# A recommender's gated experts on one core: no second layer in fp32, x rounds and second layers in one unrolled order

## The chip, the core and the metric

The kernel runs on one core of a Trainium2 chip. TensorE (PE in the profile) multiplies matrices into PSUM; VectorE (DVE), ScalarE (ACT) and GpSimd (POOL) work on tiles in SBUF and PSUM; SyncE (SP) issues transfers. Each engine runs its own instructions in order and waits for others by semaphores. The metric is the time of one execution on the device in microseconds (us).

## The reference

```
mask = x.sum(-1) != 0                                   # x: 512 x 64 x 768, fp32
p = softmax(where(mask, einsum('bld,d->bl', x, aw), -inf))
feature = einsum('bl,bld->bd', p, x)                    # 512 x 768
g_h = relu(einsum('bd,hdk->bhk', feature, gW1) + gb1)   # 4 heads, 384 wide
gate = softmax(einsum('bhk,hke->bhe', g_h, gW2) + gb2)[b, D]     # 8 experts
h1 = relu((einsum('bd,edk->ebk', feature, eW1) + eb1) * inv1 + bn1_b)   # 8 x 768 x 768
h2 = relu((einsum('ebk,eko->ebo', h1, eW2) + eb2) * inv2 + bn2_b)       # 8 x 768 x 384
rep = einsum('be,ebo->bo', gate, h2)
out = softmax((einsum('bo,hoc->bhc', rep, hW) + hb)[b, D])
```

## The kernel before

**The x rounds.** x is read once, 100 MB, in 32 rounds of 16 batch rows (four chunks of 768 KB). Eight rounds make a block of 128 batch rows, two blocks a chunk of 256. SyncE loads a round into one of four ring places when the round that held it is done (`feat_added`). In a round VectorE computes eight score tiles (`score_tile`, L637, 128x768 each) and ScalarE eight row sums for the mask (`sum_rows`, L439). Then, one round later, the softmax of the round follows: VectorE masks the scores (L645, L649), PE transposes them (`turn_scores`, L950), VectorE takes the negative maximum (L656), ScalarE the exponential (L446), VectorE normalises (L663, L665), PE transposes back (`turn_probs`, L955), VectorE places the probabilities as columns of `pwin` (`place_probs`, L678), and PE multiplies them with x (`add_features`, L972, sixteen fp32 matmuls, which the trace shows as 32 records). After eight rounds the sums are copied (`copy_rows`), transposed (`turn_features`) and split into a high and a low part in fp32r.

**The weights.** A panel is 384 columns of one weight matrix, a unit half of its rows (576 KB). GpSimd loads units. A split unit is cut by ScalarE into a high part in fp32r (`split_hi`, L423) and by VectorE into a low part (`split_lo`, L625), and PE takes three fp32r products for each tile (L908 to L910), 27 matmuls of 256 columns for a unit. ScalarE then reads the result through a relu. For a second layer h1 is also split, by VectorE (`split_h1`, L699, L701). The second layers of experts 0 to 5 of chunk 0 are the exception: their twelve units are not split, and PE multiplies raw h1 with raw weights in fp32 (`w2raw`, L940), nine matmuls for a unit, which the trace shows as 18 records.

**The order.** Three rounds' thirds and the splits of units 0 and 1 stand at the front. A loop over two blocks follows on every engine (`x_round`), with PE's `turn_scores` of the next round between the two halves of `add_features`. Then 64 slots are written out, one unit each: eight gate units of chunk 0, the experts 0 to 7 of chunk 0 with six units each (first layer in four, second in two), with the gate units of chunk 1 inside the last expert. Slots 0 to 44 each carry a third of one of the remaining x rounds (`x_third`). VectorE and ScalarE split unit s + 2 in slot s. `head_logits(0)` stands after the last slot. A second loop does chunk 1, four experts to an iteration, in the order of its layers. The vectors of parameters are transposed in slot 0 (`turn_params`, `set_params`).

Of the kernel before, what the change touches and what calls it, by code (L numbers as in the profile page):

```python
# [17 lines left out]

# [14 lines left out]
BODY = 4  # L33
EU = 6


def rec_kernel(nc, x, D, aw, gW1, gb1, gW2, gb2, eW1, eb1, bn1_g, bn1_b, eW2, eb2, bn2_g, bn2_b, hW, hb, out):
# [8 lines left out]
    GU = 2 * H  # L46
    BU = BODY * EU
    ITERS = E // BODY
    assert 2 * L == P and KT == 2 * KU and HD == UNIT_COLS and ITERS == CB
    assert MT * (NCH * GU + EU * E) // 2 % ZB == 0 and MT * (BU // 2) % ZB == 0  # L50
    assert GU % RAW == 0 and BU % RAW == 0 and BU % SPLIT == 0

# [6 lines left out]
    with ExitStack() as ctx:  # L59
# [8 lines left out]


# [60 lines left out]

        prm = rows[:, 0:2 * P].rearrange("p (a n) -> p a n", a=2)
# [7 lines left out]
        exps = soft_ps[0:ROUND_TILES, 2 * P:3 * P].rearrange("t (h l) -> t h l", h=2)  # L139

# [3 lines left out]

# [10 lines left out]
        zeroed = sem("zeroed")  # L155
        link_dve = sem("link_dve")
        params_ready = sem("params_ready")
# [16 lines left out]

        turned = sem("turned")
        turned_hi = sem("turned_hi")
        turned_read = sem("turned_read")
# [10 lines left out]
        gl_ready = sem("gl_ready")  # L188
        gmax_ready = sem("gmax_ready")
        gexp_ready = sem("gexp_ready")  # L190
        gate_ready = sem("gate_ready")
        gateT_ready = sem("gateT_ready")
# [11 lines left out]

        def tiles(it, panel, m):

            return it * (MT * BU // 2) + (MT * panel + m + 1)

        def wait_unit_used(eng, it, u0):

            if u0 % 2 == 0:
                eng.wait_ge(half_used, it * (BU // 2) + (u0 // 2 + 1))
            else:
                eng.wait_ge(z_ready, tiles(it, u0 // 2, MT - 1))


        GATES = [[(c, n, None, None) for n in range(GU)] for c in range(NCH)]
        EXPERTS = [[(0, None, q, k) for k in range(EU)] for q in range(E)]

        ORDER = (GATES[0] + [u for expert in EXPERTS[:-1] for u in expert] + EXPERTS[-1][:2] + GATES[1]
                 + EXPERTS[-1][2:])
        SLOTS = len(ORDER)

        def gate_at(c):

            return ORDER.index((c, 0, None, None))  # L230

        def expert_at(c, q, k):

            return SLOTS + EU * q + k if c else ORDER.index((0, None, q, k))

        SPLIT_FROM = 6

        def is_split(u0):  # L240
            if u0 >= SLOTS:
                return True
            _, n, q, k = ORDER[u0]
            return n is not None or k < EU - 2 or q >= SPLIT_FROM

        def splits(it, u0):

            return it * BU + sum(is_split(v) for v in range(u0 + 1))

        def h1_splits(it, c, q, t):  # L250

            return it * (KT * BODY) + (KT * (q + (E if c else 0) - SPLIT_FROM) + t + 1)

        def raw_slot(u0):

            return (splits(0, u0) - 1) % RAW

        def turned_gate(c):

            return (soft_ps if c else turn_ps)[0:E, 0:CHUNK]  # L260

        def wait_loaded(eng, it, u0):

            if is_split(u0):
                eng.wait_ge(w_loaded[raw_slot(u0)],
                            it * (16 * BU // RAW) + 16 * ((splits(0, u0) - 1) // RAW + 1))
            else:
                eng.wait_ge(w2_loaded[u0 % 2], 16 * (ORDER[u0][2] + 1))

        N1, N2 = E * KT, E * HT  # L270


        FEAT_TURN = [(2 * CB + 2) * c + (c > 0) for c in range(NCH)]
        PRM_TURN = 2 * CB

# [3 lines left out]
        GATE_TURN = [FEAT_TURN[c] + 2 * CB + (c == 0) for c in range(NCH)]  # L279

        def turned_feat(c, j, g):

            if c == 0:
                return z_ps[:, g, 0:KU * P]
            return (soft_ps if (j, g) == (CB - 1, 1) else turn_ps)[:, 0:KU * P]

        FEAT_READ = [2 * CB * c + (c > 0) for c in range(NCH)]

        SCORES, BLOCK_THIRDS = 3, 3 * BLOCK_ROUNDS

        def to_score(third):
            return range(SCORES * third, min(SCORES * third + SCORES, ROUND_TILES))


        MASK_AT, MAX_AT, NORM_AT, PLACE_AT, EXP_AT = 0, 1, 3, 4, 3

        LEAD = 3
        SLOT_THIRD = LEAD + BLOCK_THIRDS
        FIRST_SPREAD = BLOCK_ROUNDS
        ROUNDS = (1 + CB) * BLOCK_ROUNDS

        BLOCK_END = {3 * (BLOCK_ROUNDS * (j + 2) + 1) + 2 - SLOT_THIRD: j for j in range(CB)}

        BLOCK_GATED = [(t - GU) // EU for t in sorted(BLOCK_END)]

        TURN_SLOT = {(j, g): t + (g if j == 0 else 0) for t, j in BLOCK_END.items() for g in range(2)}

        GATE_COPY, GATE_PICK, GATE_NORM, GATE_SET = ([gate_at(c) + GU + n for c in range(NCH)] for n in (1, 2, 3, 4))

        block = ctx.enter_context(nc.Block())


        @block.sync  # L320
        def _(sp):
            def load_round(b, r, wait):

                if wait:
                    sp.wait_ge(feat_added, b * BLOCK_ROUNDS + (r + 1 - RING_ROUNDS))
                for j in range(CG):

                    rr, jj = divmod(r * CG + j - IN_FLIGHT, CG)
                    if (wait and j) or (rr >= 0 and not wait):
                        sp.wait_ge(x_loaded[rr % RING_ROUNDS][jj], b * 32 + 16 * (rr // RING_ROUNDS + 1))  # L330
                    sp.dma_start(xring[:, r % RING_ROUNDS, j, :, :],
                                 x_v[b, r, :, j, :, :]).then_inc(x_loaded[r % RING_ROUNDS][j], 16)

            for r in range(RING_ROUNDS):
                load_round(0, r, False)
# [12 lines left out]
            for r in range(RING_ROUNDS, BLOCK_ROUNDS):  # L348
                load_round(0, r, True)
            with sp.Fori(1, NBLK) as b:  # L350
                for r in range(BLOCK_ROUNDS):
                    load_round(b, r, True)
# [4 lines left out]


        @block.gpsimd
        def _(pool):  # L360
            nc.gpsimd.memset(ident[:, :], 0.0).then_inc(ident_zero, 1)
            pool.wait_ge(ident_zero, 1)
            nc.gpsimd.affine_select(out=ident[:, :], in_=ident[:, :], compare_op=ALU.not_equal, fill=1.0,
                                    base=0, pattern=[[-1, P]], channel_multiplier=1).then_inc(ident_ready, 1)

            def load_unit(it, u0, src):
                if is_split(u0):
                    if u0 >= RAW:

                        pool.wait_ge(lo_ready, splits(it, u0) - RAW)  # L370
                    pool.dma_start(wraw[:, raw_slot(u0), :, :], src).then_inc(w_loaded[raw_slot(u0)], 16)  # L371
                else:


                    wait_unit_used(pool, it, u0 - EU)
                    pool.dma_start(w2raw[:, u0 % 2, :, :], src).then_inc(w2_loaded[u0 % 2], 16)

            def gate_unit(u0, n):
                head, half = divmod(n, 2)
                load_unit(0, u0, gW1_v[head, :, KU * half:KU * half + KU, :])  # L380

            def expert_unit(it, u0, expert, k):
                panel, half = divmod(k, 2)
                ks = slice(KU * half, KU * half + KU)
                if panel < 2:
                    src = eW1_v[expert, :, ks, UNIT_COLS * panel:UNIT_COLS * (panel + 1)]
                else:
                    src = eW2_v[expert, :, ks, :]
                load_unit(it, u0, src)


            for r, units in ((0, range(AHEAD)), (CB * BLOCK_ROUNDS, range(AHEAD, RAW))):
                pool.wait_ge(x_loaded[r % RING_ROUNDS][CG - 1], 16 * (r // RING_ROUNDS + 1))
                for n in units:
                    gate_unit(n, n)
            for s in range(RAW, SLOTS):
                _, n, q, k = ORDER[s]
                if n is not None:
                    gate_unit(s, n)
                else:  # L400
                    expert_unit(0, s, q, k)
            with pool.Fori(0, ITERS) as it:
                for n in range(BU):
                    expert_unit(it, SLOTS + n, it * BODY + n // EU, n % EU)

            for n in range(AHEAD):
                expert_unit(0, SLOTS + BU * ITERS + n, 0, n)
            for n in range(AHEAD):
                wait_loaded(pool, 0, SLOTS + BU * ITERS + n)


        @block.scalar
        def _(act):
            act.dma_start(aw_bc[:, :], aw.partition_broadcast(P)).then_inc(aw_loaded, 16)

            def split_hi(it, u0):
                if not is_split(u0):
                    return

                wait_loaded(act, it, u0)  # L420
                if u0 >= SPLIT:
                    wait_unit_used(act, it, u0 - SPLIT)
# [725 lines left out]
```

## Time and profile before

| what | value |
|---|---|
| median of three runs | 636.95 us (636.2 to 636.99) |
| span of the profiled execution | 636.0 us |
| PE busy | 532.7 us, 84% |
| VectorE busy | 495.2 us, 78% |
| ScalarE busy | 441.0 us, 69% |
| HBM read | 168.5 MB, 265 GB/s over the span |

The span runs from the first to the last instruction of the profiled execution; the time of that execution alone was not kept, and the median of the runs is 0.95 us longer than the span. Busy shares are averages over stages with different limits, so they have to be read by stage. PEclk is the clock that TensorE was granted, 1.00 for 2.4 GHz and 0.50 for 1.2 GHz.

### The profile page before, as it was taken

Reading aid. Unit: us, or ns where it says so; the run is one execution under the profiler, and the core shown is the slowest. Engines: PE = TensorE matmul, PEld = TensorE weight load, DVE = VectorE, ACT = ScalarE, POOL = GpSimd, SP = SyncE. Lnnn points to the kernel's source line nnn. Section 1 sums busy time; section 2 is a strip of 40 time slices with the busy share of each in tenths; the row PEclk is TensorE's granted clock in tenths of the full one; section 3 lists DMA queues with packets and bytes.
Section 4 is the critical chain, followed back from the end, with each engine's and each line's share of the span. In section 5 each row is a group of like instructions: output and inputs, shape, how many; then the busy total and the mean of one; then the engine's idle time right before and its main releaser. Section 6 shows DMA issues by size and latency. Waiting matters only on the chain.

```text
span 636.0 us, 12288 instructions
## 1 busy us (share of the span) xinstructions
PE 532.7 (84%) x4153; PEld 422.3 (66%) x4153; DVE 495.2 (78%) x1085; ACT 441.0 (69%) x939; POOL 82.6 (13%) x120
## 2 busy tenths in 40 slices
PE   0075564444799999999999999999999999999994
PEld 0011111111498778787787778898899999999994
DVE  5599988999799799879798977534767677676774
ACT  5588878889698787888788885454445565555652
POOL 1000000001011210202020111111112212222210
PEclk9998885889799999999999999999989999999998
DMA  8999997999998989899989935354446655565540
GB/s 311 405 363 377 364 374 296 341 357 377 409 365 300 365 304 381 334 392 330 349 314 377 350 112 150 112 176 134 142 113 184 185 162 176 184 185 167 168 148 1
DMA packets 52618, 169.10 MB, mean 266 GB/s; under 512 B 4829, under 2 KB 5073, under 8 KB 52573
## 3 DMA queue, kind: packets, MB, share of 16 engines
q1 hardware_dynamic: 36012, 100.88, 41.7%
q0 software_dynamic: 16416, 67.25, 32.9%
q10 hardware_dynamic: 144, 0.39, 0.3%
q8 instruction: 26, 0.43, 0.3%
q14 instruction: 20, 0.16, 0.1%
HBM read 168.50 MB, written 0.00 MB: 265 GB/s over the span
## 4 chain that ended last, share of the span: by engine, by line
PE 69%; DVE 16%; issue 10%; DMA 3%; ACT 1%; DVEq 0%; SPq 0%; POOL 0%; ACTq 0%
PE z_ps L908 17%; PE z_ps L909 16%; PE z_ps L910 16%; DVE prod_out L637 10%; PE feat_ps L972 7%; PE z_ps L940 7%; DMA xring<-in_r_x_dram 2%; PE turn_ps L1039 2%; DMA wraw<-in_L_rec_gW_dram 1%; PE turn_ps L1008 1%; DVE score L637 1%; DVE neg_max L656 1%; DVE wlo L625 1%; DVE pwin L678 0%; PE turn_ps L1050 0%
## 5 line engine op out<-in xcount | busy, mean ns | idle before, releaser
L637 DVE CUSTOM_DVE_ANT_0 prod_out<-xring,aw_bc 128x768 bf16<-128x768 f32 x256 | 234.1, 948 | 5.4 <-DMA xring<-in_r_x_dram 4.7
L439 ACT ACTIVATE copy_out<-xring 128x768 bf16<-128x768 f32 x256 | 211.7, 828 | 5.8 <-DMA xring<-in_r_x_dram 5.8
L908 PE MATMUL z_ps<-feat_hi,whi 128*128 128x256 f32 x720 | 209.0, 290 | 1.5 <-DVE feat_lo L689 1.5
L909 PE MATMUL z_ps<-feat_lo,whi 128*128 128x256 f32 x720 | 204.2, 284 | 0.0
L910 PE MATMUL z_ps<-feat_hi,wlo 128*128 128x256 f32 x720 | 204.2, 284 | 0.0
L625 DVE TENSOR_TENSOR wlo<-wraw,whi 128x1152 fp32r<-128x1152 f32 x102 | 138.2, 1355 | 83.4 <-ACT whi L423 82.4
L423 ACT ACTIVATE whi<-wraw 128x1152 fp32r<-128x1152 f32 x102 | 118.3, 1160 | 86.5 <-PE z_ps L910 79.2
L908 PEld LDWEIGHTS z_ps<-feat_hi,whi 128*128 128x128 f32 x720 | 138.6, 193 | 15.8 <-issue 12.8
L909 PEld LDWEIGHTS z_ps<-feat_lo,whi 128*128 128x128 f32 x720 | 138.7, 193 | 0.0
L910 PEld LDWEIGHTS z_ps<-feat_hi,wlo 128*128 128x128 f32 x720 | 138.6, 192 | 0.0
L972 PE MATMUL feat_ps<-xring,pwin 128*32 128x384 f32 x1024 | 112.1, 573 | 12.1 <-DVE pwin L678 12.1
L371 POOL DMA_DIRECT2D wraw<-in_L_rec_eW_dram x86 | 64.3, 748 | 232.9 <-DVE wlo L625 226.3
L470 ACT ACTIVATE h<-z_ps,bias,scale 128x256 f32<-128x256 f32 x96 | 52.6, 561 | 33.7 <-PE z_ps L910 33.1
L972 PEld LDWEIGHTS feat_ps<-xring,pwin 128*32 128x32 f32 x1024 | 32.3, 120 | 60.3 <-issue 42.0
L950 PE MATMUL soft_ps<-ident,masked 128*8 128x128 f32 x32 | 9.6, 301 | 57.8 <-DVE masked L649 57.8
L908 PE MATMUL z_ps<-h_hi,whi 128*128 128x256 f32 x180 | 51.1, 284 | 0.0
L909 PE MATMUL z_ps<-h_lo,whi 128*128 128x256 f32 x180 | 50.9, 283 | 0.0
L910 PE MATMUL z_ps<-h_hi,wlo 128*128 128x256 f32 x180 | 50.9, 283 | 0.0
L950 PEld LDWEIGHTS soft_ps<-ident,masked 128*8 128x8 f32 x32 | 2.7, 84 | 72.1 <-DVE masked L649 71.3
L940 PE MATMUL z_ps<-h,w2raw 128*128 128x256 f32 x216 | 48.3, 379 | 0.0
L439 ACT ACTIVATION_READ_ACCUMULATOR copy_out<-xring 128x1 f32 x256 | 47.8, 187 | 0.0
L940 PEld LDWEIGHTS z_ps<-h,w2raw 128*128 128x128 f32 x216 | 40.1, 190 | 5.7
(99 smaller groups left out, 427.8 us busy)
## 6 DMA issues: line engine op xcount, KB each, us to landing
xring<-in_r_x_dram SPq DMA_DIRECT2D x128, 768.0 KB, 8.2
wraw<-in_L_rec_eW_dram POOLq DMA_DIRECT2D x86, 576.0 KB, 4.4
wraw<-in_L_rec_gW_dram POOLq DMA_DIRECT2D x16, 576.0 KB, 6.1
w2raw<-in_L_rec_eW_dram POOLq DMA_DIRECT2D x12, 576.0 KB, 4.6
aw_bc<-in_L_rec_aw_dram ACTq DMA_DIRECT2D x1, 384.0 KB, 5.5
w2raw<-in_L_rec_gW_dram SPq DMA_DIRECT2D x1, 48.0 KB
h<-in_L_rec_eb_dram SPq DMA_DIRECT2D x1, 24.0 KB
h<-in_L_rec_bn_g_dram SPq DMA_DIRECT2D x1, 24.0 KB
```

What stands on the lines that cost most here:

```text
L371: pool.dma_start(wraw[:, raw_slot(u0), :, :], src).then_inc(w_loaded[raw_slot(u0)], 16)
L423: nc.scalar.activation(whi[:, u0 % SPLIT, :, :], wraw[:, raw_slot(u0), :, :], ACT.Copy).then_inc(hi_ready, 1)
L439: nc.scalar.activation(copy_out[:, t % 2, :], xring[:, r % RING_ROUNDS, j, i, :], ACT.Copy, accum_out=rowsum[:, r % 2, t:t + 1]).then_inc( ...
L470: nc.scalar.activation(h1[:, t, :], z_ps[:, (MT * panel + m) % ZB, 0:CHUNK], ACT.Relu, bias=bias[:, col], scale=scale[:, col]).then_inc(z_ ...
L625: nc.vector.tensor_tensor(wlo[:, u0 % SPLIT, :, :], wraw[:, raw_slot(u0), :, :], whi[:, u0 % SPLIT, :, :].bitcast(F32), ALU.subtract).then ...
L637: nc.vector.tensor_tensor_reduce(out=prod_out[:, t % 2, :], in0=xring[:, r % RING_ROUNDS, j, i, :], in1=aw_bc[:, :], scale=1.0, scalar=0.0 ...
L908: nc.tensor.matmul(psum_tile, w_hi, a_hi, start=first, stop=False)
L909: nc.tensor.matmul(psum_tile, w_hi, a_lo, start=False, stop=False)
L910: return nc.tensor.matmul(psum_tile, w_lo, a_hi, start=False, stop=last)
L940: last = nc.tensor.matmul(z, w2raw[:, half, k, cols], h1[:, kk, :], start=(kk == 0), stop=(kk == KT - 1))
L972: last = nc.tensor.matmul(feat_ps[32 * j:32 * j + 32, half, 0:DM // 2], pwin[:, 2 * j + i, at:at + 32], xring[:, r % RING_ROUNDS, j, i, DM ...
L1039: last = nc.tensor.matmul(logit_ps[32 * head:32 * head + E, :], gW2_sb[:, HT * head + m, :], h2[:, m, :], start=(m == 0), stop=(m == HT - ...
```

## The change

- The whole program is unrolled; the two loops are gone.
- No unit is multiplied in fp32 (`NATIVE = 0`): all second layers are split and take three fp32r products, those of experts 0 to 5 of chunk 0 too, with `split_h1`, which now works on three tiles (128x768) at a time.
- The panels of an expert come in another order: the second layer of expert q - 1 (kind "c") stands between the two first-layer panels ("a", "b") of expert q, in both chunks. The gate panels of chunk 1 stand after the last expert of chunk 0.
- The weights of units 0 to 3 are loaded when round 15 of x is there, and units 0 and 1 are split at the end of round 16, no longer ahead of the rounds.
- In an x round `place_probs` moves from VectorE to ScalarE, the exponential writes `prob` in SBUF and no longer PSUM, and `turn_scores`, `turn_probs` and `add_features` of a round stand one after the other on PE. `add_features` moves from the second third of a round to the first, and the feature transposes use `feat_ps`.
- The parameters are transposed in round 10 and set before slot 0. `head_logits(0)` moves to twelve slots after the first gate unit of chunk 1.

```diff
-BODY = 4
-EU = 6
+NATIVE = 0
+THIRDS = 3
...
+        for c in range(NCH):
+            PANELS += [(c, "g", h) for h in range(H)]
+            native = NATIVE if c == 0 else 0
+            for q in range(native):
+                PANELS += [(c, "a", q), (c, "b", q), (c, "c", q)]
+            for q in range(native, E):
+                PANELS += [(c, "a", q)] + ([(c, "c", q - 1)] if q > native else []) + [(c, "b", q)]
+            PANELS += [(c, "c", E - 1)]
...
+            for r in range(FIRST_ROUNDS + 1):
+                sum_rows(r, range(0, 4))
+                if r:
+                    softmax_exp(r - 1)
+                sum_rows(r, range(4, 7))
+                if r:
+                    place_probs(r - 1)
+                sum_rows(r, range(7, ROUND_TILES))
+                if r == FIRST_ROUNDS:
+                    split_hi(0)
+                if r and r % BLOCK_ROUNDS == 0:
+                    copy_rows(r // BLOCK_ROUNDS - 1)
+                if r == FIRST_ROUNDS:
+                    split_hi(1)
...
+                nc.vector.tensor_copy(h1_hi[:, ks, :], h1[:, ks, :]).then_inc(h1_hi_ready, 1)
+                dve.wait_ge(h1_hi_ready, h1_count(c, q, half))
+                nc.vector.tensor_tensor(h1_lo[:, ks, :], h1[:, ks, :], h1_hi[:, ks, :].bitcast(F32),
+                                        ALU.subtract).then_inc(h1_ready, 1)
...
-            with pe.Fori(0, CB) as it:
-                turn_scores(it, 0)
-                for r in range(BLOCK_ROUNDS):
-                    turn_probs(it, r)
-
-                    add_features(it, r, r + 1 if r < BLOCK_ROUNDS - 1 else None)
-                for g in range(2):
-                    turn_features(it, it, 0, 0, g)
+            for r in range(FIRST_ROUNDS):
+                turn_scores(r)
+                turn_probs(r)
+                add_features(r)
+                if r % BLOCK_ROUNDS == BLOCK_ROUNDS - 1:
+                    turn_features(r // BLOCK_ROUNDS)
```

On PE at the end of the first block, before (`masked` are the scores, `prob` the probabilities, `feat_ps` the sums of a block; x8 is half of a round's products):

```order
L950 MATMUL soft_ps<-ident,masked 8x128
L972 MATMUL feat_ps<-xring,pwin 32x384 x8
L955 MATMUL soft_ps<-ident,prob 128x128
L972 MATMUL feat_ps<-xring,pwin 32x384 x16
L984 REGISTER_ALU
L993 MATMUL z_ps<-ident,rows 128x128 x6
```

The same place on PE now:

```order
L859 MATMUL soft_ps<-ident,masked 8x128
L863 MATMUL soft_ps<-ident,prob 128x128
L876 MATMUL feat_ps<-xring,pwin 32x384 x16
L889 MATMUL feat_ps<-ident,rows 128x128 x6
L859 MATMUL soft_ps<-ident,masked 8x128
```

The score transpose of a round stood between the halves of the round before and now stands behind the whole of it.

On ScalarE in a round of the first stage, now (`copy_out` and `rowsum` are the row sums; before, no row of `pwin` stands on this engine):

```order
L412 ACTIVATE copy_out,rowsum<-xring 128x768 x5
L419 ACTIVATE prob,expsum<-soft_ps,neg_max 8x64 x2
L412 ACTIVATE copy_out,rowsum<-xring 128x768 x3
L430 ACTIVATE pwin<-soft_ps 64x8 x2
L412 ACTIVATE copy_out,rowsum<-xring 128x768 x5
```

The placement stands behind the seventh sum of the next round (the last of five belongs to the round before).

On VectorE in the slots of the experts that carry x rounds, before, in two slots of expert 0 whose units ahead are not split (`prod_out` is a score tile):

```order
L656 TENSOR_REDUCE neg_max<-soft_ps 8x2
L637 ISA prod_out,score<-xring,aw_bc 128x768
L637 ISA score 128x1
L637 ISA prod_out,score<-xring,aw_bc 128x768
L637 ISA score 128x1
L637 ISA prod_out,score<-xring,aw_bc 128x768
L637 ISA score 128x1
L663 RECIPROCAL recip<-expsum 8x2
L665 TENSOR_TENSOR prob<-soft_ps,recip 8x128
L637 ISA prod_out,score<-xring,aw_bc 128x768
```

VectorE in two such slots now:

```order
L608 TENSOR_REDUCE neg_max<-soft_ps 8x2
L581 TENSOR_TENSOR wlo<-wraw,whi 128x1152
L646 CAST h1_hi<-h1 128x768
L648 TENSOR_TENSOR h1_lo<-h1,h1_hi 128x768
L593 ISA prod_out,score<-xring,aw_bc 128x768
L593 ISA score 128x1
L593 ISA prod_out,score<-xring,aw_bc 128x768
L593 ISA score 128x1
L593 ISA prod_out,score<-xring,aw_bc 128x768
L593 ISA score 128x1
L614 RECIPROCAL recip<-expsum 8x2
L616 TENSOR_TENSOR prob<-prob,recip 8x128
```

Every slot now has a low part of a weight unit, and two of every six slots the split of one half of h1.

## Rows read from the trace of the kernel before

**Rows 1.** The page, part 4: the chain that ended last, by engine.
```profile
PE 69%; DVE 16%; issue 10%; DMA 3%; ACT 1%; DVEq 0%; SPq 0%; POOL 0%; ACTq 0%
```

**Rows 2.** Windows by stage: length, busy us of each engine, PEclk, DMA share, GB/s.
```profile
25.96:157.79 131.83, 71.08 (x500) 19.08 (x500) 126.26 (x348) 110.67 (x304) 0.65 (x2) 0.83 0.95 359
157.79:171.21 13.42, 8.27 (x56) 2.88 (x56) 10.03 (x30) 8.39 (x22) 1.45 (x3) 0.75 1.02 405
171.21:220.80 49.59, 49.59 (x404) 42.22 (x405) 44.30 (x108) 42.65 (x97) 8.56 (x12) 1.00 0.94 346
220.80:383.03 162.23, 160.62 (x1241) 128.01 (x1241) 141.71 (x320) 133.03 (x309) 24.60 (x33) 1.00 0.88 323
383.03:463.06 80.03, 78.23 (x633) 69.03 (x632) 44.30 (x75) 38.98 (x60) 12.53 (x19) 1.00 0.48 147
463.06:628.59 165.53, 163.40 (x1313) 159.61 (x1312) 115.14 (x179) 94.63 (x124) 32.88 (x44) 0.99 0.53 158
```

**Rows 3.** Timeline of VectorE in one round: start, us, engine, line, operation, tiles.
```profile
57.06 0.96 DVE L637 CUSTOM_DVE_ANT_0 prod_out<-xring,aw_bc 128x768 bf16<-128x768 f32 x1
...
61.92 0.28 DVE L656 TENSOR_REDUCE neg_max<-soft_ps 8x2 f32<-8x128 f32 x1
...
64.07 0.28 DVE L665 TENSOR_TENSOR prob<-soft_ps,recip 8x128 f32<-8x128 f32 x1
...
65.15 0.34 DVE L678 COPY pwin<-soft_ps 64x8 f32<-64x8 f32 x2
...
65.52 0.96 DVE L637 CUSTOM_DVE_ANT_0 prod_out<-xring,aw_bc 128x768 bf16<-128x768 f32 x1
```

**Rows 4.** Timeline of VectorE at the start: chunks 0 and 3, first split, round 1.
```profile
7.93 0.96 DVE L637 CUSTOM_DVE_ANT_0 prod_out<-xring,aw_bc 128x768 bf16<-128x768 f32 x1 [4.66 <-DMA xring<-in_r_x_dram]
...
13.69 0.96 DVE L637 CUSTOM_DVE_ANT_0 prod_out<-xring,aw_bc 128x768 bf16<-128x768 f32 x1
...
22.19 1.36 DVE L625 TENSOR_TENSOR wlo<-wraw,whi 128x1152 fp32r<-128x1152 f32 x1 [6.65 <-ACT whi L423]
...
25.96 0.95 DVE L637 CUSTOM_DVE_ANT_0 prod_out<-xring,aw_bc 128x768 bf16<-128x768 f32 x1
```

**Rows 5.** Timeline of ScalarE in the same round: exponential, next two sums.
```profile
62.24 0.27 ACT L446 ACTIVATE soft_ps<-soft_ps,neg_max 8x64 f32<-8x64 f32 x1 [1.17 <-DVE neg_max L656]
...
62.83 0.83 ACT L439 ACTIVATE copy_out<-xring 128x768 bf16<-128x768 f32 x1
...
63.66 0.83 ACT L439 ACTIVATE copy_out<-xring 128x768 bf16<-128x768 f32 x1
```

**Rows 6.** Timeline of PE: two half bursts and the two whole bursts.
```profile
61.32 2.79 PE L972 MATMUL feat_ps<-xring,pwin 128*32 128x384 f32 x16
...
69.67 1.50 PE L972 MATMUL feat_ps<-xring,pwin 128*32 128x384 f32 x16
...
90.93 4.48 PE L972 MATMUL feat_ps<-xring,pwin 128*32 128x384 f32 x32 [0.82 <-DVE pwin L678]
...
163.63 4.29 PE L972 MATMUL feat_ps<-xring,pwin 128*32 128x384 f32 x32 [0.67 <-DVE pwin L678]
```

**Rows 7.** Timeline of PE: starts of two split units, then of two fp32 units.
```profile
242.66 0.36 PE L908 MATMUL z_ps<-feat_hi,whi 128*128 128x256 f32 x1
...
246.00 0.36 PE L908 MATMUL z_ps<-feat_hi,whi 128*128 128x256 f32 x1
...
255.55 4.05 PE L940 MATMUL z_ps<-h,w2raw 128*128 128x256 f32 x18
...
259.54 4.05 PE L940 MATMUL z_ps<-h,w2raw 128*128 128x256 f32 x18
```

**Rows 8.** Groups by form: count, busy us, mean ns, idle before and releaser.
```profile
L625 DVE TENSOR_TENSOR wlo<-wraw,whi 128x1152 fp32r<-128x1152 f32 x102 | 138.2, 1355 | 83.4 <-ACT whi L423 82.4 <-DVE gateT L812 0.2
L423 ACT ACTIVATE whi<-wraw 128x1152 fp32r<-128x1152 f32 x102 | 118.3, 1160 | 86.5 <-PE z_ps L910 79.2 <-DMA wraw<-in_L_rec_gW_dram 6.9 <-PE z_ps L940 0.4
...
L699 DVE CAST h_hi<-h 128x256 fp32r<-128x256 f32 x60 | 17.9, 298 | 3.6 <-ACT h L470 2.6
...
L725 DVE TENSOR_TENSOR rep<-rep,h 128x768 f32<-128x768 f32 x16 | 15.3, 958 | 0.5
```

More of the change, by code:

```diff
@@ L67, in sem @@
             return ctx.enter_context(nc.semaphore(name))
+        PANELS = []
+        for c in range(NCH):
[6 more added lines that the diff above has]
+            PANELS += [(c, "c", E - 1)]
+        UNITS = [(c, kind, q, half) for c, kind, q in PANELS for half in range(2)]
@@ new lines, in rec_kernel, with is_native, panel_of, unit_of @@
+        SLOTS = len(UNITS)
+        PANEL_AT = {p: n for n, p in enumerate(PANELS)}
+        def is_native(c, q):
+            return c == 0 and q < NATIVE
+        def panel_of(c, kind, q):
+            return PANEL_AT[(c, kind, q)]
+        def unit_of(c, kind, q, half):
+            return 2 * PANEL_AT[(c, kind, q)] + half
+        def is_split(u):
+            c, kind, q, _ = UNITS[u]
+            return kind != "c" or not is_native(c, q)
+        SPLITS = []
+        for u in range(SLOTS):
+            SPLITS.append((SPLITS[-1] if SPLITS else 0) + is_split(u))
@@ new lines, in rec_kernel, with raw_slot, split_slot, tiles @@
+        SPLIT_UNITS = [u for u in range(SLOTS) if is_split(u)]
+        def raw_slot(u):
+            return (SPLITS[u] - 1) % RAW
+        def split_slot(u):
+            return (SPLITS[u] - 1) % SPLIT
+        def tiles(panel, m):
+            return MT * panel + m + 1
+        SPLIT_EXPERTS = [(c, q) for c in range(NCH) for q in range(E) if not is_native(c, q)]
+        SPLIT_EXPERT_AT = {e: n for n, e in enumerate(SPLIT_EXPERTS)}
+        def h1_count(c, q, panel):
+            return 2 * SPLIT_EXPERT_AT[(c, q)] + panel + 1
@@ new lines, in before_expert, with h1_slot @@
+        def before_expert(c, q):
+            if q:
+                return c, q - 1
+            return (c - 1, E - 1) if c else None
+        def h1_slot(c, q, panel):
+            at = unit_of(c, "ab"[panel], q, 1) + 2
+            if panel == 0 and q and not is_native(c, q - 1):
+                at = max(at, unit_of(c, "c", q - 1, 0) + 2)
+            return min(at, unit_of(c, "c", q, panel) - 1)
+        H1_SLOT = {}
+        for c, q in SPLIT_EXPERTS:
+            for panel in range(2):
+                H1_SLOT.setdefault(h1_slot(c, q, panel), []).append((c, q, panel))
@@ L224, in rec_kernel @@
[L224 to L266, printed above, removed]
+        def x_count(r):
+            return 16 * (r // RING_ROUNDS + 1)
@@ L392, in _ @@
[L392 to L404, printed above, removed]
@@ new lines, in read_h1 @@
+            def read_h1(c, q, half, ms):
+                panel = panel_of(c, "ab"[half], q)
+                before = before_expert(c, q)
+                if ms[0] == 0 and before is not None:
+                    if is_native(*before):
+                        wait_unit_used(act, unit_of(before[0], "c", before[1], half))
+                    else:
+                        act.wait_ge(h1_ready, h1_count(*before, half))
+                for m in ms:
+                    t = MT * half + m
+                    read_tile(panel, m, h1[:, t, :], KT * q + t, True)
@@ L996, in gate_broadcast, with turn_features @@
-            def gate_broadcast(it, q, c):
+            def turn_features(b):
+                pe.wait_ge(rows_a, b + 1)
+                pe.wait_ge(rows_b, b + 1)
+                for g in range(2):
+                    for k in range(KU):
+                        last = nc.tensor.transpose(turned_feat(g)[:, P * k:P * k + P], rows[:, KU * g + k:DM:KT],
+                                                   ident[:, :])
+                    last.then_inc(feat_turned, 1)
+            def gate_broadcast(c, q):
```

767 lines of the change are left out of this document (337 added, 430 removed).

## The prediction

> **What bounds the kernel now.** I read the chain of work that ended last first: 69% of it is PE [rows 1]. That share mixes stages, so I cut the span at the points where the work changes and read the busy times of each stretch [rows 2]. In the rounds that come before any unit (25.96 to 157.79) VectorE is busy 126.26 of 131.83 us and PE 71.08: VectorE is the bound, a round takes 8.46 us (57.06 to 65.52 in [rows 3]), and 15 rounds make 126.9 us, so the turn from block 0 to block 1 costs the other 4.9. In slots 0 to 9 (171.21 to 220.80) PE is busy throughout. In slots 10 to 44 (220.80 to 383.03) PE is busy 160.62 of 162.23 us and VectorE 141.71, so PE is the bound and VectorE has 20.5 us of room. After that no x rounds are left, VectorE is busy little more than half of the time, and PE is the bound to the end. Before the first round VectorE stands idle until 25.96, since it must first split the weights of units 0 and 1, though the first x chunk is there at 7.93 and the fourth at 13.69 [rows 4].
>
> **The change, stage by stage.** The sum is made on the profiled span of 636.0 us; the median of the runs is 0.95 us above it, and that stays.
>
> *Start.* The first two weight loads and their splits leave the front. Four chunks land in 7.69 us at 1.92 us apart [rows 4], so the fifth is due at 15.6, and round 1 begins there and not at 25.96: -10.3 us. The loads come later, beside x rounds that VectorE and not the DMA bounds; I cost them at nothing, and if that cover failed they would cost some 3 us once.
>
> *Rounds 1 to 15.* Three edits meet here. The probabilities are placed by ScalarE after its seventh sum and not by VectorE after its fifth score, which takes 0.37 us per round off VectorE (65.15 to 65.52 in [rows 3]): its floor is 8.46 - 0.37 = 8.09. The feature products of a round run as one burst and are no longer cut in two with the next round's score transpose between the halves. That transpose now waits behind the whole burst, so a closed loop goes through every round: maximum, exponential, normalisation, transpose, placement, burst, score transpose, next maximum. Counted from a maximum (61.92 in [rows 3]): VectorE has normalised 2.43 us later (64.07 plus 0.28). ScalarE's exponential begins 0.32 after the maximum and its next sum at 0.91; three sums of 0.83 each end at 3.40 [rows 5]. The placement on ScalarE is not in this trace; two small copies lie between VectorE's 0.37 for the pair and the 0.59 of two exponentials with their read-outs, and I take 0.4, nearer to the plain copies: 3.8. With 0.06 to PE, 0.3 for the score transpose and hand-overs, the loop is 4.2 us plus the burst. A half burst takes 1.50 us at the full clock and 2.79 at half, and the two bursts that ran whole took 4.48 and 4.29, with both clocks inside [rows 6]. So the loop is 7.2 (then VectorE's 8.09 holds), 8.6 or 9.8 us. The bursts of this trace spread over all three, and a longer idle stretch follows the joined burst; I take a mean of 9.0 us, between the mixed and the slow case, with 8.09 and 9.8 as bounds. Fifteen rounds: 135.0. The turn from block 0 to block 1 puts VectorE behind the whole burst once more (3.0 us) and adds a feature subtraction of 0.5 that used to stand in the old 4.9: 3.5. Together 138.5 against 131.83: +6.7 us.
>
> A rule speaks against the joined burst. The trace shows both clocks after the same kind of pause: 61.32 slow, 69.67 fast [rows 6]. The Trainium skill, "TensorE: Matmul & The Clock Gate", section "HAM oscillation — how this bites in real kernels", says that matmuls in short groups with waits between them begin each group at half the clock again. By it only the 8.6 and 9.8 cases would occur, 9.2 on average, and the sum would come out 3 us higher; the rows above bear it out for part of the bursts only.
>
> *From round 16 to the first unit.* 13.42 us now [rows 2]. After it, the splits of units 0 and 1 stand here as well, one of them between the copy of the feature rows and the feature subtractions: 11.9 us to the end of the copy (3.0 to the maximum, three of the eight scores and the mask, then 3.8, a burst of 4.5, 0.6), 1.2 and 1.3 for the split, 1.0 for the subtractions, 15.4 in all: +2.0 us.
>
> *Slots 0 to 9.* PE has the same ten units; the parameter transposes leave and one burst is due earlier. VectorE sets the parameters ahead of slot 0, which makes PE wait there about as long as the transposes took. I take 0, with 2 us either way.
>
> *Slots 10 to 44.* Twelve fp32 units become split units. On PE a split unit takes 3.34 us and an fp32 unit 3.99, each with its transpose [rows 7]: 12 x 0.65 = 7.8 us less work. But VectorE gets 12 more low parts of 1.355 us (16.3), and 12 splits of a half of h1, each a cast and a subtraction of 128x768. A subtraction of that size is taken at the 0.96 of the sum of two 128x768 tiles [rows 8]. The cast has no row of that size; it lies between one cast of 128x256 (0.30) and three (0.89) [rows 8], I take 0.65, since fixed cost is paid once: 12 x 1.61 = 19.3. Off go eleven placements (0.34 busy each, 3.7) and one gate product with its sum (0.96 each, 1.9), as the last second layer falls out of the stretch. VectorE's work is then 141.7 + 16.3 + 19.3 - 3.7 - 1.9 = 171.7 us, more than the 162.23 that the stretch takes now, and PE's falls to about 153. So VectorE becomes the bound. ScalarE goes from 133.0 by 12 x 1.16 [rows 8] and 11 x 0.4 to 151, under both. For waits in order I add 1.5%, 2.5 us: before, VectorE had no long waits where it was the bound. PE ends slot 44 about 2.5 us ahead of VectorE. 174.2 - 2.5 = 171.7 against 162.2: +9.5 us. Bounds: the short cast and no wait give +3, the long cast and 5% of waits +19.
>
> *Between the chunks of 256 rows.* Now PE waits 1.8 us at the head products of chunk 0 [rows 2], since they stand behind the last expert's sum, and its clock dips after (0.99 over the next 165 us). After, they stand 13 slots later among units. A new short wait may arise where the first gate panel needs h2 free. I take -2 us, between -3.5 and 0.
>
> *The rest.* The late second layer changes nothing where no x rounds run: six units and a broadcast leave PE no gap today either (163.40 of 165.53, the remainder at the tail), and VectorE has room. Unrolled code costs nothing in slots 0 to 9 today, so I take none later.
>
> Sum: -10.3 + 6.7 + 2.0 + 9.5 - 2.0 = +5.9. Span 641.9, median **643 us**.
>
> **Rivals.** (1) *The head start wins.* If the joined bursts run mostly at the full clock, rounds come to 8.3: stage one gives -10.3 - 3.8 + 1.5, and with no waits in slots 10 to 44 (+7.0) and -2 the median is 629. It decides below 8.6 us a round, where stage one's gain equals the rest. For it: the half bursts at 1.50; against it: both whole bursts above 4.2 [rows 6].
> (2) *Every burst begins slow* after the longer pause and often stays so to its end: 9.6 us a round, which is +9 on stage one: 652. For it: the slow half burst at 61.32; against it: the fast one at 69.67 after the same pause. The rule of the Trainium skill named above points this way.
> (3) *Three engines in lockstep.* In slots 10 to 44 VectorE at 100%, ScalarE and PE near 90% of the time wait on one another in program order, 8% on VectorE's work: +11, 654. For it: VectorE's low parts already wait on ScalarE's high parts [rows 8]; against it: in slots 0 to 9 all three are above 85% and PE loses nothing [rows 2].
> (4) *The fp32 units' saving shows whole*, VectorE's new work hidden: -7.8 in place of +9.5, 626. VectorE's sum excludes it unless an operation is far cheaper than its row. That the fp32 products stay is ruled out: none stands in the new order.
>
> **How the numbers follow.** Forecast, 638.3 to 650: 0.52. Rival 2: 0.09, rival 3: 0.07, together 0.16. About 0.2% is what a measurement of this kernel can tell from no change; within it, where stage one's gain and slots 10 to 44 cancel: 0.12. Rival 1: 0.17, rival 4: 0.03, together 0.20. So slower 0.68, same 0.12, faster 0.20. The range runs from 631, into rival 1, to 657, past rivals 2 and 3.
>
> **What the new profile would show.** Round 1 at 15.6 us; a round of about 9 us with VectorE waiting for PE ahead of its maximum; the first unit at about 169.6; in slots 10 to 44 VectorE busy over 95% and PE under 92%; slot 44 done at about 391; no PE wait between the chunks. I am wrong if rounds come to 8.1, if the h1 cast is far from 0.65, or if VectorE waits there for more than 5%.

## The result

The changed kernel takes **645.2 us** (median of 4 runs, 644.3 to 646.73) against 636.97 us of the kernel before on the same chip: 1.013 times as long, 95% interval 1.0113 to 1.0147. The forecast was 643. The profiled execution has a span of 643.6 us, 7.6 above the 636.0 of before.

The page of the changed kernel, busy times of the engines and the chain that ended last (its first line answers to [rows 1]):

```profile
PE 538.9 (84%) x4261; PEld 427.9 (66%) x4261; DVE 498.0 (77%) x975; ACT 460.2 (72%) x1013; POOL 81.2 (13%) x118
...
PE 45%; DVE 23%; issue 6%; ACT 2%; ACTq 0%; DVEq 0%
```

The shares can't be set against the 69% and 16% of before as they stand: this chain could be followed back only to 152.8 us, so its shares sum to 76% and leave out rounds 1 to 15. What they show is that behind that point, where the units run, 23% of the span now hangs on VectorE. In which stretch, the windows by stage tell. Here they are cut where the same work begins in both kernels: first score of round 1, first score of round 16, first product of slot 0, of slot 11, of slot 47, of slots 55, 64 and 73, and the end of the last unit. ([rows 2] had its cuts for the slots at 220.80 and 383.03, inside a round; before slots 11 and 47 equally many bursts are done in both kernels.) The kernel before: window, length, busy us of PE, PEld, VectorE, ScalarE and GpSimd, PEclk, DMA share, GB/s.

```profile
171.21:224.01 52.80, 52.80 (x439) 43.52 (x439) 47.31 (x118) 43.21 (x101) 8.56 (x12) 1.00 0.95 349
224.01:392.51 168.50, 166.89 (x1296) 134.26 (x1292) 146.40 (x326) 138.20 (x317) 25.90 (x35) 1.00 0.85 311
392.51:424.46 31.95, 31.95 (x268) 28.64 (x264) 15.40 (x23) 16.36 (x23) 4.47 (x8) 1.00 0.45 141
424.46:462.92 38.46, 36.66 (x280) 32.70 (x280) 21.21 (x37) 16.89 (x27) 6.75 (x9) 1.00 0.50 152
462.92:494.44 31.52, 31.52 (x247) 31.05 (x247) 22.47 (x41) 17.37 (x25) 5.98 (x8) 0.95 0.51 147
```

The changed kernel, the same stages, with those ahead of the first unit:

```profile
0.00:15.38 15.38, 0.00 (x0) 0.00 (x0) 9.38 (x20) 8.33 (x17) 0.69 (x6) 1.00 0.88 314
15.38:154.32 138.94, 80.53 (x505) 24.66 (x509) 120.12 (x318) 116.69 (x334) 2.28 (x4) 0.74 0.98 375
154.32:170.88 16.56, 10.26 (x68) 3.44 (x60) 12.24 (x29) 12.34 (x29) 1.06 (x2) 0.71 1.03 402
170.88:225.07 54.19, 53.90 (x426) 44.63 (x427) 46.44 (x111) 44.41 (x106) 7.07 (x10) 0.94 0.84 298
225.07:399.41 174.34, 161.52 (x1403) 134.06 (x1401) 167.02 (x330) 152.87 (x351) 27.65 (x37) 0.99 0.84 302
399.41:431.55 32.14, 30.71 (x260) 28.17 (x258) 20.88 (x26) 17.85 (x26) 4.93 (x8) 1.00 0.48 149
431.55:467.33 35.78, 35.02 (x264) 31.15 (x264) 13.93 (x11) 15.57 (x22) 6.12 (x9) 1.00 0.50 150
467.33:502.02 34.69, 33.47 (x269) 31.71 (x268) 21.45 (x40) 18.02 (x30) 6.52 (x9) 1.00 0.51 150
```

Stage by stage, with the forecast beside it (us; the first three rows of before are in [rows 2] or, for the start, its end point 25.96):

| stage | forecast | measured |
| --- | --- | --- |
| start, to round 1 | -10.3 | 15.38 - 25.96 = -10.6 |
| rounds 1 to 15 | +6.7 | 138.94 - 131.83 = +7.1 |
| round 16 to the first unit | +2.0 | 16.56 - 13.42 = +3.1 |
| first slots (to slot 11) | 0 | 54.19 - 52.80 = +1.4 |
| slots 11 to 46 | +9.5 | 174.34 - 168.50 = +5.8 |
| slots 47 to 72, the turn of the chunks | -2.0 | 102.61 - 101.93 = +0.7 |
| rest | 0 | 0 |
| sum | +5.9 | +7.6 |

From slot 73 to the end both kernels take the same time to 0.02 us.

### The profile page after: what moved, and what is told of

The parts are those of the page before. It is cut to its first block, busy times and chain, and to the rows that moved or that the text cites. A ratio compares the mean times of both kernels' runs of the same rounds, so it can differ in the third digit from the quotient of the medians.

```text
span 643.6 us, 11454 instructions
## 1 busy us (share of the span) xinstructions
PE 538.9 (84%) x4261; PEld 427.9 (66%) x4261; DVE 498.0 (77%) x975; ACT 460.2 (72%) x1013; POOL 81.2 (13%) x118
## 4 chain that ended last, share of the span: by engine, by line
PE 45%; DVE 23%; issue 6%; ACT 2%; ACTq 0%; DVEq 0%
PE z_ps L819 13%; PE z_ps L820 12%; PE z_ps L821 12%; DVE prod_out L593 10%; DVE wlo L581 7%; PE feat_ps L876 4%; PE turn_ps L908 2%; DVE h_hi L646 1%; DVE h L666 1%; PE turn_ps L900 1%; ACT whi L397 1%; DVE h_lo L648 1%; ACT copy_out L412 1%; PE turn_ps L921 0%; DVE score L593 0%
## 5 line engine op out<-in xcount | busy, mean ns | idle before, releaser
L581 DVE TENSOR_TENSOR wlo<-wraw,whi 128x1152 fp32r<-128x1152 f32 x112 | 151.4, 1352 | 87.9 <-ACT whi L397 87.9
L397 ACT ACTIVATE whi<-wraw 128x1152 fp32r<-128x1152 f32 x112 | 129.8, 1159 | 73.8 <-PE z_ps L821 73.7
L448 ACT ACTIVATE h<-z_ps,bias,scale 128x256 f32<-128x256 f32 x144 | 78.7, 559 | 36.1 <-PE z_ps L821 35.9
L819 PE MATMUL z_ps<-h_hi,whi 128*128 128x256 f32 x288 | 82.7, 287 | 3.1 <-ACT h L448 1.6
L820 PE MATMUL z_ps<-h_lo,whi 128*128 128x256 f32 x288 | 81.4, 283 | 0.0
L821 PE MATMUL z_ps<-h_hi,wlo 128*128 128x256 f32 x288 | 81.4, 283 | 0.0
L819 PEld LDWEIGHTS z_ps<-h_hi,whi 128*128 128x128 f32 x288 | 55.2, 192 | 4.2 <-ACT h L448 2.6
L820 PEld LDWEIGHTS z_ps<-h_lo,whi 128*128 128x128 f32 x288 | 55.2, 192 | 0.0
L821 PEld LDWEIGHTS z_ps<-h_hi,wlo 128*128 128x128 f32 x288 | 55.2, 192 | 0.0
L863 PE MATMUL soft_ps<-ident,prob 128*128 128x128 f32 x32 | 11.2, 349 | 50.9 <-DVE prob L616 50.9
```

Source lines behind the costliest of these rows:

```text
L397: nc.scalar.activation(whi[:, split_slot(u), :, :], wraw[:, raw_slot(u), :, :], ACT.Copy).then_inc(hi_ready, 1)
L448: ins = nc.scalar.activation(dest, src, ACT.Relu, bias=bias[:, col:col + 1], scale=scale[:, col:col + 1])
L581: nc.vector.tensor_tensor(wlo[:, split_slot(u), :, :], wraw[:, raw_slot(u), :, :], whi[:, split_slot(u), :, :].bitcast(F32), ALU.subtract) ...
L819: nc.tensor.matmul(psum_tile, w_hi, a_hi, start=first, stop=False)
L820: nc.tensor.matmul(psum_tile, w_hi, a_lo, start=False, stop=False)
L821: return nc.tensor.matmul(psum_tile, w_lo, a_hi, start=False, stop=last)
```

## The experiments

All are made on the changed kernel, and each was timed beside the kernel before on its chip; a ratio is that to the kernel before. Where a stage is the question I compare the stage in the traces, since the time of the whole also holds how many bursts of rounds 1 to 15 met the slower clock, and that differs between executions (one fast burst of sixteen in the trace of the changed kernel, two in that of the kernel with six experts in fp32, whose rounds ahead of the units are the same).

**The loop of a round.** The first experiment cuts the loop that the forecast put at 4.2 us plus the burst.

```diff
                 for i in range(2):
+                    if i and ahead is not None:
+                        turn_scores(ahead)
...
-                turn_scores(r)
+                if r % BLOCK_ROUNDS == 0:
+                    turn_scores(r)
                 turn_probs(r)
-                add_features(r)
+                add_features(r, r + 1 if (r + 1) % BLOCK_ROUNDS else None)
```

> The changed kernel with one thing undone: in rounds 1 to 15, inside a block, the score transpose of the next round stands between the two halves of a burst of feature products again. Theory A (the loop maximum, exponential, normalisation, transpose, placement, whole burst, score transpose sets a round at 4.2 us plus the burst): the loop is cut, VectorE's own work of 8.1 us sets a round, rounds 1 to 15 take 122 to 126 us and not 138.9, the whole about 631 us. Rival B (the placement on ScalarE or the loading of x sets a round): rounds stay above 8.8 us, the whole above 640.

Measured: 634.92 us, ratio 0.9967 (0.9948 to 0.9987); rounds 1 to 15 take 127.98 us, where the changed kernel takes 138.94. VectorE's waits in that stretch (line, who ended the wait, us in all, times, longest), first of the changed kernel, then of this one:

```profile
DVE neg_max L608 <- PE soft_ps L859: 13.6, 12, 2.2
DVE rows L622 <- PE feat_ps L876: 4.1, 1, 4.1
```

```profile
DVE rows L622 <- PE feat_ps L878: 4.7, 1, 4.7
DVE prod_out L593 <- DMA xring<-in_r_x_dram: 2.8, 4, 1.7
```

The wait of the maximum for the score transpose is gone, 13.6 us of it, and most rounds take 7.89 us. Theory A holds, B falls: the placement still stands on ScalarE. But the gain in the stage is 11 us and not the 13 to 17 expected, since another bound stands right behind: VectorE now waits for x itself, 2.8 us in all. In this window 390 GB/s are moved at a DMA share of 1.02; stretches of 16 us in it reach 404. A round is four loads of 768 KB, 3.15 MB, or 7.8 us at 404 GB/s.

**The clock as the reason for the long burst.** Here the order of the changed kernel stays, and TensorE is kept at work in its pauses; the added products write to a part of PSUM that is not yet in use, and nobody reads them.

```diff
...
                 turn_scores(r)
+                fill(4)
                 turn_probs(r)
+                fill(1)
                 add_features(r)
```

> The changed kernel with idle stretches of TensorE in the x rounds filled: four fp32 products of 128x256 that nobody reads between the score transpose and the transpose of the probabilities, one more ahead of the burst. Theory A with the clock as the reason for the long burst: the burst falls from a mean of 4.8 us to about 2.8, the loop to 7.0, VectorE's 8.1 us sets the round, the whole is about 631 us. Rival C (the burst is long for another reason, and only its place matters): bursts stay near 4.8, the added products delay what stands behind them by up to 1 us a round, the whole is 645 to 660.

Measured: 635.7 us, ratio 0.998 (0.996 to 1.0); rounds 1 to 15 take 130.85 us. Windows of rounds 1 to 15, first with the burst cut in halves, then with the filled pauses:

```profile
15.19:143.17 127.98, 70.37 (x505) 20.30 (x509) 119.38 (x318) 117.61 (x334) 2.28 (x4) 0.83 1.02 390
```

```profile
15.34:146.19 130.85, 97.38 (x659) 47.09 (x663) 119.64 (x318) 117.22 (x334) 2.28 (x4) 0.92 1.03 390
```

The granted clock of the stage rises from 0.74 to 0.92, with 17 us more of PE's work. PE's bursts in three rounds of it:

```profile
64.87 2.79 PE L876 MATMUL feat_ps<-xring,pwin 128*32 128x384 f32 x32 [0.55 <-ACT pwin L430]
72.75 2.79 PE L876 MATMUL feat_ps<-xring,pwin 128*32 128x384 f32 x32 [0.55 <-ACT pwin L430]
80.79 4.40 PE L876 MATMUL feat_ps<-xring,pwin 128*32 128x384 f32 x32 [0.70 <-ACT pwin L430]
```

Eight of the sixteen bursts now take 2.79 us, where the changed kernel has one, and most rounds behind such a burst take 7.9. The other eight still take 4.3 to 4.6: the filling was not enough to hold the clock in each round. So the clock is what makes the burst long (rival C falls), and the expected 631 was missed by the rounds in which it still fell: VectorE's wait of the maximum for the score transpose is still there in six rounds, 5.8 us of it.

**VectorE's work in the slots with x rounds.** Two experiments bring back fp32 units and leave the order of rounds as it is; the layers c of the experts named stand directly behind their a and b then, so each of the two undoes two things, the split and the late layer. The experiment after them undoes the late layers alone.

```diff
-NATIVE = 0
+NATIVE = 2
```

> The changed kernel with the second layers of experts 0 and 1 of chunk 0 in fp32 again (4 units of 12). Theory D (VectorE's added work sets the slots of the experts with x rounds): VectorE loses 4 x (1.35 + 1.51) = 11.4 us of 167 there, TensorE gains 2.6 on 161.5, both come to 157 to 165, the stretch from slot 11 to slot 47 falls from 174.3 to about 167, the whole to about 638 us. Rival E (the order of late second layers or of the round's thirds makes the stretch long, not VectorE's work): TensorE's 2.6 us come on top, about 648.

Measured: 637.8 us, ratio 1.0034 (1.0008 to 1.006).

```diff
-NATIVE = 0
+NATIVE = 6
```

> The changed kernel with the second layers of experts 0 to 5 of chunk 0 in fp32 again, all twelve units, as before the change; the order of rounds stays. Theory D: VectorE loses 34 us and is no longer the bound, TensorE has 161.5 + 7.8 = 169.3 us of work, the stretch falls from 174.3 to 168 to 170, the whole to about 640 us. Rival E: the stretch grows by 7.8 us, the whole to about 653.

Measured: 636.52 us, ratio 1.0001 (0.9976 to 1.0027). The stretch from slot 11 to slot 47 in the two, first with two experts in fp32, then with six:

```profile
221.01:389.86 168.85, 162.56 (x1366) 133.19 (x1365) 156.59 (x316) 149.48 (x348) 26.14 (x35) 1.00 0.84 305
```

```profile
223.70:390.35 166.65, 166.65 (x1294) 133.57 (x1293) 137.18 (x293) 142.78 (x340) 26.07 (x35) 1.00 0.85 309
```

The stretch falls from 174.34 to 168.85 and 166.65 us, although PE's work grows from 161.52 to 162.56 and 166.65. With six experts PE doesn't idle in it at all and is the bound again. Theory D holds within 2 us, E falls in both. The second line also tells what the rest of the change is worth in this stretch without the new work: 166.65 against 168.50 of the kernel before, which has the same twelve fp32 units with the same order of layers.

**The late second layers.**

```diff
+            if c == 0:
+                for q in range(E):
+                    PANELS += [(c, "a", q), (c, "b", q), (c, "c", q)]
+                continue
```

> The changed kernel with the late second layers undone in chunk 0: there each expert takes its panels a, b and then c, as before the change; all split. Theory D (VectorE's work, which stays the same, sets the slots with x rounds): the stretch from slot 11 to slot 47 keeps its 174 us within 2, the whole stays at 643 to 648 us. Rival F (the late order hides the wait of TensorE for the split of h1, some 1.5 us of VectorE's work and its queue, in each expert): 5 experts with x rounds and 2 to 3 without lose 1 to 2 us each, the whole is 651 to 660.

Measured: 647.84 us (644.56 to 651.74), ratio 1.017 (1.0115 to 1.0224). As a time this can't be told from the changed kernel. In the trace the stretch from slot 11 to slot 47 takes 176.31 us, 2.0 more, and slots 47 to 54, where no x is left, 33.22, 1.1 more. D is right on what sets the stretch; without the late layers the two stretches take some 3 us more, less than F asked for. So the gain of the two experiments before comes from the fp32 units, since undoing the late layers alone costs time.

**The head start.**

```diff
-                if u in (0, 2):
-                    r = FIRST_ROUNDS - 1
-                    pool.wait_ge(x_loaded[r % RING_ROUNDS][0 if u == 0 else CG - 1], x_count(r))
...
-                if r == FIRST_ROUNDS:
-                    split_hi(0)
+                if r == 0:
+                    split_hi(0)
```

and the same for the other three splits.

> The changed kernel with the weights of units 0 to 3 loaded at once and units 0 and 1 split behind round 0, as before the change. If the head start is worth what it shows and the later loads cost nothing beside the rounds: round 1 begins some 10 us later (about 26 and not 15.4), the rounds stay as they are, the way from round 16 to the first unit falls from 16.6 to about 13.5, the whole is about 652 us. If the later loads collide with x, the rounds fall too, and the whole is 646 to 649.

Measured: 653.02 us, ratio 1.0249 (1.0223 to 1.0274). Windows of the start, of rounds 1 to 15 and from round 16 to the first unit:

```profile
0.00:24.56 24.56, 0.00 (x0) 0.00 (x0) 11.94 (x23) 11.96 (x23) 3.50 (x11) 1.00 0.94 349
24.56:163.04 138.48, 80.53 (x505) 24.72 (x509) 120.10 (x319) 114.97 (x332) 0.53 (x1) 0.74 0.97 366
163.04:178.67 15.63, 10.27 (x68) 3.45 (x61) 9.62 (x27) 9.45 (x26) 0.00 (x0) 0.71 0.92 342
```

Round 1 begins 9.2 us later, and the rounds keep their 138.5 us: beside these rounds the later loads cost 0.5 us at most. The way to the first unit falls by 0.9 only, not by 3: where the split of unit 1 stood, VectorE now waits for ScalarE's high part of the features.

```profile
177.59 1.02 DVE L624 TENSOR_TENSOR feat_lo<-feat_ps,feat_hi 128x384 fp32r<-128x384 f32 x2 [1.35 <-ACT feat_hi L436]
```

**Putting the gains together.** Two kernels keep the head start and the late layers of the experts that stay split, cut every burst but the last, take some experts back to fp32, and move the copy of block 0's sums out of the way of VectorE and ScalarE at the turn of the blocks.

```diff
+                late = r > BLOCK_ROUNDS and r % BLOCK_ROUNDS == 1
+                if late:
+                    copy_rows(r // BLOCK_ROUNDS - 1)
                 score_tiles(r, range(3, 5))
...
-                add_features(r)
+                add_features(r, r + 1 if r + 1 < FIRST_ROUNDS else None)
...
-NATIVE = 0
+NATIVE = 6
```

> The changed kernel with three edits: the second layers of experts 0 to 5 of chunk 0 in fp32 again; every burst but the last cut in halves around the next score transpose, at the turn from block 0 to block 1 too; and the copy of the feature rows of block 0 moved from the end of round 8 to behind the maximum of round 9, so that VectorE and ScalarE don't wait there for the whole burst. If the gains add: 11 us from the halves, 4 from the turn (13.1 to about 9 us) and 8 from the fp32 units, about 622 us. If the loading of x (3.1 MB a round at 401 GB/s, 7.84 us) takes the place of the turn's wait, the turn gives nothing: about 626.

Measured: 625.19 us, ratio 0.9814 (0.9796 to 0.9833).

> The same three edits with experts 0 to 3 in fp32 (8 units of 12). VectorE's work in the slots with x rounds is then 167 - 22.8 = 144 us and TensorE's 161.5 + 5.2 = 166.7 with the waits gone: the stretch is 167 us as with twelve units or 1 to 2 less, the whole 621 to 623.

Measured: 624.69 us, ratio 0.9801 (0.9779 to 0.9824), the fastest kernel of this study by its median; the two can't be told apart, and 621 to 623 was not reached. Rounds 1 to 15, the way to the first unit and slots 11 to 46 of the last:

```profile
15.48:139.98 124.50, 72.56 (x513) 20.48 (x513) 119.42 (x320) 117.16 (x334) 2.28 (x4) 0.83 1.03 394
139.98:159.33 19.35, 10.45 (x61) 3.10 (x57) 12.33 (x27) 13.06 (x29) 1.06 (x2) 0.59 1.03 403
212.20:379.09 166.89, 164.33 (x1331) 133.22 (x1329) 146.42 (x304) 145.97 (x344) 26.11 (x35) 1.00 0.85 308
```

The rounds come down to 124.5 us at a DMA share of 1.03, and what the turn gave there is taken back on the way to the first unit, which grows to 19.35 us. From round 1 to the first unit it is 143.85 us with the turn mended and 143.93 with the halved bursts alone (15.19 to 159.12). VectorE's waits for x from the start of round 16 on:

```profile
DVE prod_out L600 <- DMA xring<-in_r_x_dram: 3.3, 3, 1.9
```

So the loading of x has become the bound there, as the second of the two expectations had it (0.7 of the 3.3 us lie just ahead of the stretch). That the first four weight units, which are loaded at the same time, are what delays x is argued: no run moves them in this kernel. With eight fp32 units PE has 2.6 us of room in the slots and VectorE 20.5.

## Why the prediction was right, and where it was not

The direction was right, and so were the two costs that the sum rests on, the longer rounds behind a joined burst and VectorE's new work in the slots. That the sum came out only 1.7 us too low is in part luck: slots 11 to 46 were put 3.7 us too high, and the rounds, the way to the first unit, the first slots and the turn of the chunks together 5.6 us too low.

**Start.** Right: 15.38 against 15.6. That the later loads cost nothing was right in this kernel, to the 0.5 us that early loads changed the rounds by. The forecast put some 3 us on them if the cover failed; in the fastest kernel, with shorter rounds, VectorE waits 2.6 us for x on the way to the first unit, and that way takes 2.8 us more (19.35 against 16.56). That agrees with the condition, and doesn't prove it.

**The loop.** Right in mechanism and size. VectorE's maxima and PE in the same round of the changed kernel (start, us, engine, line, operation, tiles, and the idle time ahead of it):

```profile
54.59 0.28 DVE L608 TENSOR_REDUCE neg_max<-soft_ps 8x2 f32<-8x128 f32 x1 [1.26 <-PE soft_ps L859]
...
64.07 0.28 DVE L608 TENSOR_REDUCE neg_max<-soft_ps 8x2 f32<-8x128 f32 x1 [1.50 <-PE soft_ps L859]
```

```profile
57.07 0.33 PE L863 MATMUL soft_ps<-ident,prob 128*128 128x128 f32 x1 [2.52 <-DVE prob L616]
58.38 5.35 PE L876 MATMUL feat_ps<-xring,pwin 128*32 128x384 f32 x32 [0.98 <-ACT pwin L430]
63.66 0.38 PE L859 MATMUL soft_ps<-ident,masked 128*8 128x128 f32 x1
66.55 0.33 PE L863 MATMUL soft_ps<-ident,prob 128*128 128x128 f32 x1 [2.52 <-DVE prob L616]
67.86 4.39 PE L876 MATMUL feat_ps<-xring,pwin 128*32 128x384 f32 x32 [0.98 <-ACT pwin L430]
```

From the maximum at 54.59 to the burst at 58.38 it is 3.79 us (3.8 forecast), the burst takes 5.35, and the next maximum follows at 64.07: 9.48 us, the burst plus 4.13. The burst that ran at the full clock throughout is this one, and it is the only one of sixteen; the others took 4.13 to 5.35 us, 4.8 on average with it:

```profile
117.50 2.79 PE L876 MATMUL feat_ps<-xring,pwin 128*32 128x384 f32 x32 [0.98 <-ACT pwin L430]
```

The 13 rounds clear of the turn average 8.9 us against the 9.0 taken, so the turn of the blocks costs 138.94 - 15 x 8.9 = 5.4 us and not 3.5: two small errors against each other. Rivals 1 and 2 were decided by that average: short rounds needed less than 8.6, and bursts that all begin slow and often stay so to their end needed 9.6. The Trainium skill, "TensorE: Matmul & The Clock Gate", section "HAM oscillation — how this bites in real kernels", says that short groups with waits between them begin each group at half the clock. Fifteen of the sixteen bursts here agree, the one at 2.79 us does not, and the average came out below the 9.2 us that the rule was worth: 4.8 us for a burst, where 9.2 less the loop's 4.2 is 5.0. That activity in the pauses brings the clock back is what the filled kernel showed, 0.92 against 0.74.

VectorE's own floor was put at 8.09 us a round and is 7.89: I took the placement's 0.37 off a round of 8.46 that also held 0.2 us of short gaps.

**From round 16 to the first unit.** The burst there took 5.31 us where 4.5 was taken, and the maximum came 0.5 us later; these two make up the miss (+3.1 against +2.0). The split between the copy and the subtractions took 2.3 us, where 2.5 was taken. What the sum left out is that it takes the place of another wait: without it VectorE waits 1.35 us for the features' high part, so taking it out gave 0.9 us.

**First slots.** Forecast 0, measured +1.4, of which 1.05 is in slot 0: 5.99 us against 4.94. The first unit of each kernel, window and busy times as above, first of before, then of the changed one:

```profile
171.21:176.15 4.94, 4.94 (x42) 4.77 (x42) 4.22 (x10) 4.03 (x9) 0.53 (x1) 1.00 1.03 402
```

```profile
170.88:176.87 5.99, 5.99 (x28) 5.92 (x29) 5.85 (x23) 1.91 (x6) 0.53 (x1) 0.50 1.03 404
```

Before, the transposes of the parameters follow the unit in that slot, all at the full clock; now the unit is alone in it, at a granted clock of 0.50. The work left and the clock took its place. The forecast had put a wait for VectorE's setting of the parameters there, and PE has none in the slot (5.99 us busy of 5.99).

**Slots 11 to 46.** Right on the mechanism: VectorE is busy 167.02 of 174.34 us, 96%, and PE 161.52, 93%. The size was too large, +9.5 against +5.8. VectorE's work was put 30 us higher and rose by 20.6 (146.40 to 167.02). Groups of the changed kernel in this stretch: count, busy us, mean ns, idle time before.

```profile
L581 DVE TENSOR_TENSOR wlo<-wraw,whi 128x1152 fp32r<-128x1152 f32 x37 | 49.7, 1342 | 0.0
L648 DVE TENSOR_TENSOR h_lo<-h,h_hi 128x768 fp32r<-128x768 f32 x13 | 12.5, 959 | 0.4
...
L646 DVE CAST h_hi<-h 128x768 fp32r<-128x768 f32 x13 | 7.0, 542 | 0.0
```

The cast takes 0.54 us where 0.65 was taken, 1.3 us in 12. The subtraction is at its 0.96. The Trainium skill, "VectorE: DVE Perf Modes", section "The perf-mode tier table (the rule you actually need)", lists a copy of fp32 in SBUF at twice the rate of an operation on two fp32 tensors; 0.54 against 0.96 us agrees. The largest part, 5.1 us, is in how the durations were added: on an engine that doesn't wait, one instruction begins before the last one's duration is over. In this stretch the listed durations of all groups sum to some 161 us before and 187 after, a rise of 25.7, and the engine was busy 146.40 and 167.02. So twelve times 1.355 and 0.96 overstate what the work adds; the distance from one start to the next (1.27 for a low part, 0.88 for a score tile) is nearer to the price. Most of the rest is that this stretch, cut one slot later than the forecast's, has 11 more low parts and not 12, and that 2.4 us of casts and subtractions of 128x256 left it. VectorE's waits were taken at 2.5 us and were 7.3 (174.34 - 167.02), most of it two waits of a maximum for its transpose:

```profile
DVE neg_max L608 <- PE soft_ps L859: 5.8, 2, 3.4
```

Rival 3, lockstep, needed waits of 8% of VectorE's work; 7.3 us is 4.4%, so the forecast took too little for waits and the rival too much. Rival 4 is ruled out by the fp32 experiments: the saving of the fp32 units never shows, since taking them back makes the kernel faster.

**The turn of the chunks.** The step that failed: -2.0 forecast, +0.7 measured. PE's waits from 392 to 500 us before:

```profile
PE turn_ps L1050 <- DVE rep L725: 1.8, 1, 1.8
```

That wait, at the head products, is gone, as forecast. PE's waits from 399 to 510 us in the changed kernel, slot 47 to some units behind slot 73, are three:

```profile
PE z_ps L819 <- DVE h_lo L648: 1.4, 1, 1.4
PE turn_ps L935 <- DVE gate L714: 1.2, 1, 1.2
PE z_ps L819 <- ACT h L450: 0.8, 1, 0.8
```

That is 3.4 us in place of 1.8; PE's work in the stretch falls by 0.9 us (100.13 to 99.20), and the two make the +0.7. Of the three, the forecast named only the last, the first gate panel that needs h2 free: ScalarE reads it out behind the sum of the last expert. The first is at the last expert's second layer, which has no later panel ahead of it and waits for the split of h1. At the second, the gate of chunk 1 is normalised on VectorE behind the split of h1 in the same slot, and PE waits for it in order; the gate of chunk 0 makes PE wait 3.9 us in slots 11 to 46 in the same way, where VectorE is the bound. I read this from the trace; no run here moved these instructions.

## What to carry to other kernels

A burst that is joined into one piece can lengthen a loop through several engines: add up the loop from one instruction to the same one a round later, with the burst at the clock it will be granted, before counting what the joined order saves. A cheaper form on one engine is worth nothing where it hands its work to another that has less room: the same stretch took 174 us with no fp32 unit, 169 with four and 167 with eight or twelve. Price added work by the distance between starts of like instructions, not by their durations.

## What was not expected of the hardware

With the pauses filled, the two clock levels follow one another from burst to burst though the added products are the same: 2.79 us in half of the rounds and 4.3 to 4.6 in the others. What differs is how long TensorE idles ahead of the second transpose. After a slow burst it was 0.8 us inside a block, and the next burst was fast in all seven cases; after a fast one it was 1.7 to 2.0 us, and the next burst was fast in one case of seven. One transpose of each kind, ahead of the bursts at 64.87 and 80.79:

```profile
63.56 0.33 PE L863 MATMUL soft_ps<-ident,prob 128*128 128x128 f32 x1 [0.79 <-DVE prob L616]
79.33 0.33 PE L863 MATMUL soft_ps<-ident,prob 128*128 128x128 f32 x1 [1.86 <-DVE prob L616]
```

No run varies this idle time alone. And the loads of x are close behind VectorE in the first stage: the busiest of the 40 slices of each page shows 403 to 409 GB/s, which is 7.7 to 7.8 us for a round, against VectorE's 7.89.
